# Sixteen unread products per merged turn, placed ahead of three waits of TensorE

## The reference

```python
x = x + _L0_attn_ref(_layernorm(x), ...)              # a whole encoder: 4 layers, linear attention and feed-forward
x = x + _L0_xattn_ref(_layernorm(x), ctx, ctx, ...)   # 16 heads of 8, softmax, masked
x = x + _L0_ffn_ref(_layernorm(x), ...)               # quantized, depthwise convolution between two products
x = x + _L1_attn_ref(_layernorm(x), ...)              # 16 heads; each row keeps its 64 largest scores
x = x + _L1_xattn_ref(_layernorm(x), ctx, ctx, ...)   # attention over channels
x = x + _L1_ffn_ref(_layernorm(x), ...)               # 8 experts, all of them used
```

```python
h = _layernorm(x, ln1_s, ln1_b)
q, k, v = h @ Wq + bq, h @ Wk + bk, h @ Wv + bv
qp, kp = elu(q) + 1, elu(k) + 1
kv, ksum = sum_s kp v, sum_s kp                       # per head
x = x + (qp kv / (qp ksum + eps)) @ Wo + bo
x = x + relu(_layernorm(x, ln2_s, ln2_b) @ W1 + b1) @ W2 + b2
```

## Time and profile before

| | |
|---|---|
| Median of 3 runs | 1364.49 us |
| The profiled execution | 1363.77 us |
| Its span | 1362.0 us |
| TensorE (PE) busy | 1034.4 us, 76% |
| VectorE (DVE) busy | 961.6 us, 71% |
| ScalarE (ACT) busy | 669.4 us, 49% |
| GpSimd (POOL) busy | 488.1 us, 36% |
| Granted TensorE clock, mean | 0.848 |

### The profile page before, as it was taken

The page is one execution under the profiler, slowest core; times in us unless marked ns, Lnnn a source line. Parts: engine busy times, 40 slices in busy tenths (PEclk is TensorE's granted clock), DMA queues, the critical chain, the costliest instruction groups (busy, mean ns, idle before and its releaser), DMA issues.

```text
span 1362.0 us, 17932 instructions
## 1 busy us (share of the span) xinstructions
PE 1034.4 (76%) x5103; PEld 682.6 (50%) x5106; DVE 961.6 (71%) x3098; ACT 669.4 (49%) x1768; POOL 488.1 (36%) x461
## 2 busy tenths in 40 slices
PE   5898846555768288875766589779888856878999
PEld 4777623334445166553533334433444445657787
DVE  7665588977488788888867868455777777774332
ACT  4444336443667256664337544247666643632322
POOL 4333266411655145555246400424343422331100
PEclk9999958867888668887668898889888987989999
DMA  4101110000000000000010011011110121222443
GB/s 142 29 23 31 31 31 1 1 0 1 13 20 15 1 18 14 18 10 1 1 54 1 1 39 47 24 47 51 55 47 24 51 78 39 82 74 72 137 142 114
DMA packets 41762, 53.88 MB, mean 40 GB/s; under 512 B 6448, under 2 KB 20672, under 8 KB 41664
## 3 DMA queue, kind: packets, MB, share of 16 engines
q1 hardware_dynamic: 41488, 52.24, 12.3%
q0 software_dynamic: 176, 0.53, 0.1%
HBM read 51.71 MB, written 1.05 MB: 39 GB/s over the span
## 4 chain that ended last, share of the span: by engine, by line
PE 46%; DVE 32%; POOL 8%; issue 7%; ACT 5%; DVEq 1%; DMA 0%; POOLq 0%; SPq 0%; ACTq 0%
PE psum L1747 7%; PE psum L1758 7%; PE psum L1733 6%; PE psum L1514 3%; DVE near L2060 3%; PE psum L1333 2%; PE psum L1410 2%; PE psum L1490 2%; PE psum L1837 2%; POOL Wk L711 2%; PE psum L1830 2%; DVE S L2565 2%; DVE smax L2570 2%; DVE Wk L2070 1%; DVE h L1974 1%
## 5 line engine op out<-in xcount | busy, mean ns | idle before, releaser
L2272 DVE TENSOR_TENSOR big<-psum,qe 128x512 f32<-128x512 f32 x106 | 73.0, 689 | 145.7 <-PE psum L1758 74.2
L1040 ACT ACTIVATE far<-far,half_far,fmul 128x128 bf16<-128x128 bf16 x256 | 104.2, 485 | 27.9 <-DVE hit L2047 27.9
L1193 ACT ACTIVATE qe<-psum 128x512 f32<-128x512 f32 x106 | 62.5, 592 | 102.2 <-PE psum L1747 100.6
L1733 PE MATMUL psum<-big,wexp 128*128 128x256 f32 (+1 forms) x340 | 112.5, 445 | 0.0
L766 POOL TENSOR_TENSOR Wk<-Wk,far 128x1024 f32<-128x1024 f32 x32 | 70.2, 2193 | 94.4 <-ACT far L1040 94.4
L2060 DVE MAX8 near<-Wk 128x8 f32<-128x128 f32 x512 | 103.0, 276 | 0.0
L668 POOL TENSOR_SCALAR veps<-mv 128x4 f32<-128x4 f32 x35 | 8.8, 252 | 255.8 <-DVE mv L1966 255.8
L1410 PE MATMUL psum<-ident,Wk 128*128 128x128 f32 x256 | 47.6, 354 | 48.5 <-POOL Wk L711 46.6
L1733 PEld LDWEIGHTS psum<-big,wexp 128*128 128x128 f32 x340 | 67.6, 199 | 29.0 <-issue 21.0
L1758 PE MATMUL psum<-xin,wexp 128*128 128x512 f32 x128 | 69.9, 629 | 13.9 <-DVE far L2272 7.8
L1747 PE MATMUL psum<-xin,wexp 128*128 128x512 f32 x128 | 75.2, 672 | 1.5 <-DVE vaug L2712 1.5
(11 more groups left out here) (361 smaller groups left out, 2830.7 us busy)
## 6 DMA issues: line engine op xcount, KB each, us to landing
wexp<-in_mg SPq DMA_DIRECT2D x48, 256.0 KB, 2.6
wexp<-in_mu SPq DMA_DIRECT2D x48, 256.0 KB, 3.0
wexp<-in_md SPq DMA_DIRECT2D x48, 256.0 KB, 3.0
w<-in_aw SPq DMA_DIRECT2D x8, 256.0 KB, 2.8
w<-in_w2a SPq DMA_DIRECT2D x8, 256.0 KB, 2.6
wqkv<-in_aw SPq DMA_DIRECT2D x8, 192.0 KB, 2.2
ctxt<-in_ctx SPq DMA_DIRECT2D x5, 256.0 KB, 4.3
xin<-in_x SPq DMA_DIRECT2D x4, 256.0 KB, 2.9
```

Of the source, the lines that this page charges most:

```text
L1040: ins = act.activation(far[t][:, hd, :], far[t][:, hd, :], ACT.Identity, bias=half_far[:, 0:1], scale=fmul[t][:, hd:hd + 1])
L1733: mm = pe.matmul(bank(4)[:, 0:w], wd[l % 2][:, c + j, :], hid_of[k >= EARLY][k % CH][:, j * w:(j + 1) * w], start=first and j == 0, stop=l ...
L2272: dve.tensor_tensor(hid_of[k >= EARLY][k % CH], bank(U_BANK[k]), sg_of[k >= EARLY][k % 2], ALU.mult).then_inc(hu_done, 1)
```

## The change

A helper `unread(to, n)` issues n products of `ident` by `ident`, 128 x 128 x 128 in float32, into one bank. Nobody reads them; the next product in that bank writes over them. It is called at three places in the merged turns:

```diff
@@ attend(k, part)
                 if part == "input":
+                    if k == 1:
+
+                        pe.wait_ge(lin_done, both(0, i + 1))
+                    if k >= 2:
+                        unread(6, 6)
                     pe.wait_ge(ln_h, 2 * norm_no("A", k)[0])
-                    if k == 1:
-
-                        pe.wait_ge(lin_done, both(0, i + 1))
                     transposes(bank(6), h_of("A", k), ident[:, :], hT_mm, 2)
@@
                 if part == "attention":
                     pe.wait_ge(q_pos, both(s, i + 1))
+                    if k >= 1:
+                        unread(5, 6)
                     pe.wait_ge(kv_sum, both(s, i + 1))
@@
+            def unread(to, n):
+
+
+                for _ in range(n):
+                    pe.matmul(bank(to)[:, 0:P], ident[:, :], ident[:, :], start=True, stop=True)
+
             def feed(k, part):
@@ feed(k, "input")
                     transposes(bank(6), h_of("F", k), ident[:, :], hT_mm, 2)
+                    if k + 1 < STEPS:
+                        unread(7, 4)
```

More of the change, by code:

```diff
@@ L1552, in attend @@
                 if part == "input":
-                    pe.wait_ge(ln_h, 2 * norm_no("A", k)[0])
                     if k == 1:
                         pe.wait_ge(lin_done, both(0, i + 1))
+                    if k >= 2:
+                        unread(6, 6)
+                    pe.wait_ge(ln_h, 2 * norm_no("A", k)[0])
                     transposes(bank(6), h_of("A", k), ident[:, :], hT_mm, 2)
```

## The result

The changed kernel took 1352.66 us, the median of 4 runs (1348.10 to 1372.35), against 1366.42 us for the kernel before (4 runs, 1363.63 to 1370.68). The ratio is 0.9898 with a 95% interval of 0.9854 to 0.9943, so the change makes the kernel about 1% faster. Five more rounds gave 0.9911 (0.9881 to 0.9941). Forecast were 5.4 us; the change is worth 12 to 14. Its profiled execution took 1350.60 us with a span of 1348.8.

What follows compares the result with a forecast made beforehand. No engine was full: a ring of handovers bound the merged turns, TensorE's clock mattering only where VectorE waits for it. Gains per place summed to 5.9 us, less 0.5 for late starts, 5.4: 1358.4 us, range 1352.5 to 1367.

Steps and rivals of the forecast that it cites:

- 0.88 was asked for: Sign of being right: TensorE's clock over the merged turns rises from 0.79 to 0.88 or more.
- the three waits of kk: VectorE's waits for the projections, 1.33, 1.04 and 0.57 us in b = 0, 3, 4, were to fall under 0.3.
- that of xs: VectorE's wait for the product down, 2.81 and 1.84 us in b = 3 and 4, was to fall to 1.3.
- the charge for late starts: 0.5 us taken off the sum for the input's six unread products ending late, 0.36 us on average at 2.4 GHz.
- Turn 1: Gain from the input of b = 0, where kk waits 1.33 us: 1.1 us taken, bounds -0.4 and 1.3.
- Turns 5 to 7: Input of b = 4, 0.5 us (0 to 0.6), and all other turns, 0.3 us (-0.5 to 1.0).
- Outside the merged turns no instruction changes: Step that gave the code outside the merged turns no term in the sum.
- The rule weighed: Rule that only long waits between bursts lose the clock, so filling short waits brings nothing; time as the first rival's, 1362.5 us.
- (1): Merged turns: the clock doesn't follow the filling, or VectorE absorbs TensorE's gain; 1362.5 us, chance 0.22.
- (2): Merged turns: all upper bounds hold, 8.0 us, and turned scores and exponentials come some 2 us earlier; 1354 us, chance 0.12.
- (3): Merged turns: unread products run at 1.2 GHz and push what stands behind them, overrunning by 9 us; 1371 us, chance 0.11.

Runs made afterwards that it cites:

- thin: The changed kernel with its 106 unread products cut to 10 moving columns instead of 128; 1.0067 to the kernel before.
- att_only: The changed kernel with only the six unread products ahead of kv_sum in the attention (42 in all); 1.0011 to the kernel before.
- inp_only: The changed kernel with only the input's six unread products, ahead of the wait for the normalized tile (36 in all); 0.9974 to the kernel before.
- hold_more: The changed kernel plus 12 unread products in the untouched stretch, four ahead of at in every merged turn, 6 and 8 in turn 6; 0.9938 to the kernel before.
- shift: The kernel before with VectorE finding five heads' second eight twice in turn 8, a delay of 1.1 us in the profile; 0.9975 to the kernel before.
- before_hold: The kernel before with 12 unread products only in the untouched stretch, at the cross queries; 0.9942 to the kernel before.
- after_shift: The changed kernel with VectorE finding 11 heads' second eight twice in turn 8, a delay of 2.5 us in the profile; 1.0016 to the kernel before.
- after: The first profile of the changed kernel, nothing else altered; execution 1350.6 us.
- again: The whole change once more, unaltered, in five more rounds with a second profile; 0.9911 to the kernel before, profiled execution 1350.7 us.
- after2: A third profile of the changed kernel, nothing else altered; execution 1357.0 us.
- after_hold: The changed kernel plus 12 unread products in the untouched stretch, at the cross queries; 0.9942 to the kernel before.
- after_shift_hold: The changed kernel with the delay of 11 heads in turn 8 and 12 unread products in the untouched stretch; 0.9945 to the kernel before.
- tail_after: The changed kernel plus 46 unread products in TensorE's waits behind the merged turns that the change fills; 0.9930 to the kernel before.

## Why the prediction came out half as large

**The mechanism** in the merged turns was right: products in these waits raise the clock, and VectorE's waits shrink. The clock rose to 0.86 (0.88 was asked for), the three waits of kk went, that of xs fell to 1.28 in b = 3 and 4, L1582 takes 1.15 to 1.25 us in b = 0, 4 and 5, and the busy time of TensorE hardly grew (1034.4 to 1036.0 us with 212 more rows). `thin` shows that the same products with 10 columns, which leave the clock at 0.79, gain nothing. What was wrong is that each place has a gain of its own: `att_only` was worth 3 us by my sum and gave nothing, and `inp_only` has longer merged turns.

**The sum over the merged turns** came out right, in part by luck. From one xs to the next, by the start of the line, before and after:

| to xs of turn b | before | after | difference | forecast for it |
|---|---|---|---|---|
| 0 (from kk) | 18.6 | 17.5 | -1.1 | -1.0 |
| 1 | 31.0 | 31.7 | +0.7 | -1.1 |
| 2 | 31.9 | 32.2 | +0.3 | none |
| 3 | 60.6 | 59.9 | -0.7 | -1.3 |
| 4 | 35.1 | 33.1 | -1.9 | -1.7 |
| 5 | 34.0 | 32.4 | -1.6 | -0.5 |
| 6, 7 | 73.0 | 71.4 | -1.6 | -0.3 |

Together -6.0 us against -5.9 before the charge for late starts. Turn 1 is the largest miss among them. The kk at the end of turn 0 no longer waits, but the gain was lost in turn 1: VectorE's den and at come only behind its own 16 replacements (MATCH_REPLACE8), TensorE waits 2.80 us for them instead of 1.04, the clock falls, and the product down takes 5.37 us instead of the 3.74 of a turn at 2.4 GHz. The unread products that `hold_more` puts ahead of this wait leave 1.91 us of it; the clock falls there all the same and down takes 5.37 us. In the profile of the changed kernel:

```profile
394.31 0.66 PE L1333 MATMUL psum<-ident,at 128*128 128x128 f32 x4 [2.80 <-DVE at L2403]
394.81 5.37 PE L1628 MATMUL psum<-w,big 128*128 128x128 f32 x32
```

Turns 5 to 7 gave more than I had for them. I had taken one profile of before as typical; in the second, turns 5 and 6 are 34.4 and 35.1 us instead of 34.0 and 32.9. And in `shift` and `before_hold`, whose code is the kernel before's up to turn 7, the first row is 16.9 us instead of 18.6 and turn 1 is 32.3 instead of 31.0. So single terms of the table are as large as what one execution of the kernel before differs from another, and -1.1 in the first row isn't the change's alone. The gain of all merged turns is 6 to 7 us by the profiles of either kernel.

**The step that failed** is the sentence "Outside the merged turns no instruction changes", from which I took the rest at nothing. No instruction changes there, but the clock does, and the stretch behind the last drop gave 5.9 us, as much as the whole sum. The changed kernel comes out of its last merged turn at a moment from which the clock holds through the cross queries and most of L1514, in all three profiles of it, and the kernel before at one from which it doesn't, in both: 27 against 33 us. With this the sum is 7.3 + 5.9 = 13.2 us, by the means of five profiles; the start gives another 1.6 and the end 0.7, and the rounds say 12 to 14. Shown by runs is that the stretch is worth 5 to 6 us by the clock alone (`before_hold`), and that a delay of 2.5 us takes it from the changed kernel (`after_shift`). Why the changed kernel arrives at the good moment in each profile is not shown, nor that it does so in every execution: of its fourteen in the two sets of rounds, eleven took 1347 to 1360 us and three 1368 to 1372, and none of the three was profiled. What the profiles have is that its turns 0 to 6 repeat to 0.1 us in six executions (`after`, `again`, `after2`, `after_shift`, `after_hold`, `after_shift_hold`), although the clock's first change comes at 16.4 us in one and at 18.0 to 19.8 in the others; it looks as if the work falls into step with the clock. It doesn't always: in `tail_after`, whose code is the same up to there, turns 3 and 6 took 3.1 and 4.4 us longer. The 1.6 us at the start lie ahead of every edit and are chance as far as five profiles tell: other kernels with the same code there have both values.

**The rule weighed.** The Trainium skill, "TensorE: Matmul & The Clock Gate", "HAM oscillation — how this bites in real kernels", ties the loss to long waits between bursts. One fall in the trace agrees: in both kernels the clock is at 1.2 GHz through most of the wait of 23 us ahead of L1572. The others don't: with waits of 0.66 to 3.3 us filled with products the clock rose from 0.79 to 0.86. Part 1 of the same page of the Trainium skill says that how many products run at 1.2 GHz differs from run to run of one kernel; here the trace agrees: the second profile of the kernel before has a stretch at 1.2 GHz from 553.5 to 557.0 us that the first hasn't, and the two executions differ by 8.9 us, 2.7 of them in the merged turns.

**Rivals.** (1), no gain: its ground, that VectorE absorbs it, was wrong by the rows of xs and kk in b = 0, 3 and 4, and right in b = 1. The 1.3 us that its time stands on are worked out nowhere in the prediction. (2), everything holds, at 1354 us, is nearest in time, but for another reason than I gave. (3) is what `thin` measured. The forecast range of 1352.5 to 1367 had the median of 1352.66 in it by a hair, and only with the execution of 1372.35 us; the median of the other three is 1350.60. Its low end came from the merged turns alone and had no room for the rest of the kernel.

## What to carry to other kernels

Where TensorE's clock falls beside short waits, unread dense products in these waits can be worth their time, if the neighbouring waits get some too: one place alone left the merged turns at 422.9 us or more here, against 423.2. More isn't always better; `hold_more` filled further waits and gained nothing. When work on the chain is moved by a few microseconds, look for thin work on TensorE (products with few columns) behind the last edit and price it at both clocks; in this kernel that was as much as the change itself. Take more than one profile of the kernel before, since one execution shows only one way in which the clock can fall.

## What was not expected of the hardware

- 2.5 us more work cost 9 us between the profiles and 11 to 14 by the executions (0.9911 to 1.0016, `after_shift`), and twelve unread products of 128 columns brought part of it back (0.9945).
- Runs of the kernel before spread from 1358.4 to 1372.8 us in one set of rounds. Whole parts that no edit touches take one of three lengths, whichever kernel it is: from the first to the eighth masked tile of the first cross attention 56.9 to 57.4, 59.1 to 59.4, or 61.3 to 62.0 us, and VectorE's last part, behind the last drop of the second half, 120.7, 122.3 or 123.9 to 124.1.
- Six unread products of 10 columns take TensorE 1.46 us at 2.4 GHz and six of 128 columns 1.56. The median weight load is 192 ns in both; whether it sets this time no run shows. Only with the 128 columns did the clock rise (0.86 against 0.79).
